# Queue of the two maximum transfers in four attention layers: from SyncE to GpSimd

## The reference

```
logits = einsum('bqhd,bkhd->bhqk', q, k) * scale + bias or mask
w      = softmax(logits)                 # exp(l - max(l)) / sum
out    = einsum('bhqk,bkhd->bqhd', w, v)
```

## Time and profile before

| | |
|---|---|
| median of 3 runs | 2353.46 us (2351.25 to 2359.56) |
| the profiled execution | 2350.0 us, its span 2348.3 us |
| TensorE busy | 2052.1 us, 87% of the span |
| VectorE busy | 1544.7 us, 66% |
| ScalarE busy | 1199.0 us, 51% |
| GpSimd busy | 825.0 us, 35% |
| DMA issues | all by SP; shift_dram<-rows x64 (24 KB), st<-shift_dram x128 (12 KB) |

### The profile page before, as it was taken

The page is one execution under the profiler, slowest core; times in us unless marked ns, Lnnn a source line. Parts: engine busy times, 40 slices in busy tenths (PEclk is TensorE's granted clock), DMA queues, the critical chain, the costliest instruction groups (busy, mean ns, idle before and its releaser), DMA issues. The chain is left out here.

```text
span 2348.3 us, 52692 instructions
## 1 busy us (share of the span) xinstructions
PE 2052.1 (87%) x20735; PEld 1381.5 (59%) x20735; DVE 1544.7 (66%) x2742; ACT 1199.0 (51%) x2044; POOL 825.0 (35%) x1272
## 2 busy tenths in 40 slices
PE   6999999999959997998689989997599985479996
PEld 3666666666648995555578966664345543335553
DVE  5777777777743435666354447774688875768884
ACT  3444444444343324665623326655477776447774
POOL 4444444444423432332144414441233322433330
PEclk9999999999969998999789989998699997769998
DMA  5000000000000022444000214441244420134441
GB/s 167 1 1 1 1 1 1 1 1 1 1 6 2 14 46 70 113 113 99 2 4 1 55 29 113 113 112 32 70 100 115 113 61 1 42 80 107 113 109 46
DMA packets 142787, 120.97 MB, mean 52 GB/s; under 512 B 11808, under 2 KB 127408, under 8 KB 142548
## 3 DMA queue, kind: packets, MB, share of 16 engines
q1 hardware_dynamic: 142548, 117.64, 21.1%
HBM read 63.48 MB, written 54.12 MB: 50 GB/s over the span
## 5 line engine op out<-in xcount | busy, mean ns | idle before, releaser
L906 DVE TENSOR_REDUCE l_group_mx<-maxima 128x4 f32<-128x1024 f32 x248 | 304.0, 1226 | 69.0 <-PE maxima L699 67.5
L834 ACT ACTIVATE l_group_pr<-scores 128x1024 f32<-128x1024 f32 x256 | 261.5, 1021 | 71.7 <-PE scores L720 69.1
L2171 POOL TENSOR_TENSOR l_wide_tiles_sum<-l_wide_pr 128x256 f32<-128x256 f32 x256 | 180.7, 727 | 212.4 <-ACT l_wide_pr L2114 212.4
L2142 DVE RECIPROCAL l_wide_rc<-bank 128x256 f32<-128x256 f32 x128 | 223.8, 1749 | 8.4 <-PE bank L2075 7.9
L2114 ACT ACTIVATE l_wide_pr<-scores 128x512 f32<-128x512 f32 x256 | 139.1, 595 | 163.1 <-PE scores L2058 163.1
L2126 DVE TENSOR_REDUCE l_wide_mx<-maxima 128x2 f32<-128x512 f32 x248 | 159.4, 685 | 52.6 <-PE maxima L2038 52.0
L906 DVE TENSOR_REDUCE l_slope_mx<-maxima 128x6 f32<-128x768 f32 x124 | 118.9, 959 | 74.2 <-PE maxima L706 72.7
L2104 ACT ACTIVATE l_wide_qk<-bank 128x512 f32<-128x512 f32 x128 | 76.4, 597 | 175.2 <-PE bank L2025 175.2
L906 DVE TENSOR_REDUCE l_rope_mx<-maxima 128x6 f32<-128x768 f32 x124 | 118.8, 958 | 56.3 <-PE maxima L706 55.4
L834 ACT ACTIVATE l_slope_pr<-scores 128x768 f32<-128x768 f32 x128 | 103.5, 809 | 87.0 <-PE scores L727 86.8
L834 ACT ACTIVATE l_rope_pr<-scores 128x768 f32<-128x768 f32 x128 | 103.7, 811 | 77.0 <-PE scores L727 76.8
(11 more groups left out here) (468 smaller groups left out, 4853.5 us busy)
## 6 DMA issues: line engine op xcount, KB each, us to landing
l_group_st<-stack_dram SPq DMA_DIRECT2D x64, 384.0 KB, 5.5
l_slope_st<-stack_dram SPq DMA_DIRECT2D x32, 384.0 KB, 5.6
l_rope_st<-stack_dram SPq DMA_DIRECT2D x32, 384.0 KB, 5.5
stack_dram<-l_group_parts SPq DMA_DIRECT2D x64, 192.0 KB, 2.3
stack_dram<-l_group_parts SPq DMA_DIRECT2D x64, 128.0 KB, 1.9
stack_dram<-l_slope_parts SPq DMA_DIRECT2D x32, 192.0 KB, 2.4
stack_dram<-l_rope_parts SPq DMA_DIRECT2D x32, 192.0 KB, 2.3
stack_dram<-l_slope_parts SPq DMA_DIRECT2D x32, 128.0 KB, 2.3
```

The costliest lines, as they stand in the source:

```text
L834: act.activation(pr[:, i % AHEAD, :, 0:keys], Tp[:, :, 0:keys], ACT.Exp).then_inc(s["exps"], 1)
L906: dve.tensor_reduce(mx[:, b % 2, :, :, i], max_bank(i, b)[:, :, 0:BLOCKS * keys].rearrange("p z (a k) -> p z a k", k=keys), AX.X, ALU.max, ...
L2142: own.done(dve.reciprocal(rc[:], Ob[i % 2][:, S:2 * S]))
L2171: pool.tensor_tensor(tiles_sum[:, i % 2, z, :], pr[:, i % 2, z, 0:S], pr[:, i % 2, z, S:2 * S], ALU.add).then_inc(s["added"], 1)
```

## The change

The steps "shift" and "spread" leave SP's lists and are issued by GpSimd, through the same function, with the same waits and semaphores. In slope and rope they follow "parts" of the same period; in group "shift" comes ahead of "reg_q" and "parts", and "spread" after them. High, mid, low and stack stay with SP in their order.

```diff
@@ slope
-            [("parts", 0, 3)],
-            [],
-            [],
+            [("parts", 0, 3), ("shift", 0, 1)],
+            [],
+            [("spread", 0, 1)],
             [],
         ],
         "sp": [
...
-            [("shift", 0, 1), ("high", 0, 3)],
+            [("high", 0, 3)],
             [("mid", 0, 3)],
-            [("spread", 0, 1), ("low", 0, 3)],
+            [("low", 0, 3)],
@@ rope
             [("parts", 0, 3)],
-            [],
-            [],
+            [("shift", 0, 1)],
+            [("spread", 0, 1)],
             [("bias", 0, 1)],
...
-            [("shift", 0, 1), ("high", 0, 3)],
-            [("spread", 0, 1)],
+            [("high", 0, 3)],
+            [],
             [("mid", 0, 3), ("low", 0, 3)],
@@ group
             [("split", 0, 1), ("bias", 0, 1)],
-            [("reg_q", 0, 2), ("parts", 0, 3)],
-            [],
+            [("shift", 0, 1), ("reg_q", 0, 2), ("parts", 0, 3)],
+            [("spread", 0, 1)],
             [("reg_v", 0, 2)],
...
-            [("shift", 0, 1), ("high", 0, 3)],
-            [("spread", 0, 1)],
+            [("high", 0, 3)],
+            [],
             [("mid", 0, 3), ("low", 0, 3)],
@@ pool_piece
-            if what == "split":
+            if what in ("shift", "spread"):
+                sp_piece(pool, what, i, b)
+            elif what == "split":
```

## The result

The changed kernel takes 2619.03 us (median of 4 runs, 2614.16 to 2623.87) against 2352.36 us before: ratio 1.1121, 95% interval 1.11 to 1.1143. That is 267 us slower, in the direction that was forecast, twice the forecast size and outside the range. Its profiled execution has a span of 2616.3 us with a mean granted clock of 0.892, against 2348.3 us and 0.932 before.

A forecast was written before the change was run, and what follows sets the result against it. TensorE's in-order stream sets the time, with a late score 0 paid once a period. Slope 24, rope 33, group 70 make 127 us, plus 8 for layers' last periods: +135, so 2488 us; range 2395 to 2560.

The forecast's parts named there:

- the chain: From GpSimd free for the shift to score 0: shift landing, semaphore, two spreads; 5.70 us in slope and rope.
- The cost d of an issue: Time one transfer issue holds GpSimd, three a period; taken as 1.04 us, the sum moving 168 us per us of d.
- The small power on 128x4: GpSimd instruction on 128x4 elements, nearly all its own software; its 1.04 us was taken as the cost of an issue.
- The landing of the spread: Second spread's start to score 0's weight load: 1.79 us from SP in slope, 2.49 with GpSimd's issue cost.
- rival 4: Gaps of 2 to 3 us a period might lower TensorE's clock: +64, 2552; chance 0.14, shared with a dearer issue.
- Rival 3: SP's queue is the brake; freed, stack lands earlier and TensorE's 27.1 us of waits go: 2327; chance 0.06.
- Rivals 1 and 2: Issues cheap as SP's; 1: landings 0.4 us longer, 2405, chance 0.12; 2: landings as early, 2360, chance 0.08.

## Why the prediction was wrong

**What held.** The direction and its reason: score 0 waits for the spread in nearly every period (57 waits), the stack's waits go, the shift stands where I placed it. Without the collision the chain is the one I drew: in group the shift starts 9.54 us behind score 0 (2453.27 to 2462.81; forecast 9.26), and from the shift to score 0 it is 2470.23 - 2462.81 = 7.42 us (forecast 8.65). The periods of group are 16.9 us in the quiet ones and 17.3 in the mean, against 17.91 forecast and 15.41 before.

**The cost d of an issue.** Taken as 1.04 us, measured 0.51 to 0.57. The small power on 128x4 was the wrong neighbour. This alone would have made the forecast too high, by 168 x 0.5 = 84 us. Group came out 10 us a layer below the forecast; by d alone it would have been 14 x 3 x 0.5 = 21, so other terms took half of that back. The error in d and the one that follows pull in opposite directions, and the total hides a part of the larger one.

**The landing of the spread: the step that failed.** I took 1.79 us from one pair in slope and added 0.70. That row is a landing with the stack not yet issued. I moved the shift, and the spread with it, 2.1 us later and did not ask what SP would be sending by then, though the stack's place stands in my own text and its size, twice 384 KB, on the page. The slope period by its terms:

| term | forecast | measured |
|---|---|---|
| score 0 to the end of parts | 10.57 | 11.7 |
| shift start to spread start | 2.17 | 2.4 |
| first spread's issue | 1.04 | 0.5 |
| second spread to score 0 | 2.49 | 6.5 |
| period | 16.3 | 21.1 |

(measured: score 0 at 1087.47, the shift at 1099.09, score 0 at 1108.53.) The landing is 4.0 of the 4.8 us. Over all periods of slope the medians of the four terms are 11.6, 2.4, 0.5 and 6.3 us. In rope they are 13.3, 2.4, 0.5 and 6.6, against 11.46, 2.17, 1.04 and 2.49: the landing is 4.1 us too long there, and the stretch up to the parts 1.9. Holding the stack back took 123 us from the time, out of the 214 of slope and rope; the later chain and the lower clock go with the rest, and were not parted.

**The clock, rival 4.** I gave it a small chance because a gap of about 2 us in group had kept it at 1.00. In group that held for most periods: between the first and the last shift of a layer the mean is 0.94 and 0.95, against 0.97 before. In slope and rope it is 0.80, down from 0.97 and 0.98:

```profile
906.00:1218.00 312.00, 208.54 (x3064) 134.71 (x3068) 140.09 (x236) 130.10 (x207) 85.27 (x159) 0.80 0.32 73
1495.00:1827.00 332.00, 230.14 (x3182) 153.70 (x3182) 156.18 (x267) 129.33 (x210) 110.23 (x186) 0.80 0.30 69
```

TensorE's extra 59 us of busy time for the same products are what a row shows of its size. So rival 4 was not instead of my forecast but on top of it, in slope and rope. In three of the experiments gaps of 1.8 to 2.1 us in slope were followed by the lower clock too (0.57 in a window behind the gap at 1060.86 in the one with the shift ahead of the parts), where one of 1.9 us in group was not, as these windows around the group's score 0 at 2470.23 show; what else decides it is open.

```profile
2466.00:2470.00 4.00, 2.32 (x30) 1.23 (x26) 3.71 (x8) 1.35 (x3) 2.77 (x5) 1.00 0.54 150
2470.00:2474.00 4.00, 3.72 (x46) 2.15 (x46) 1.91 (x5) 2.75 (x5) 0.00 (x0) 1.00 0.63 119
```

**Rival 3, SP as the brake,** is refuted by the sign. What SP gained in room was worth at most the 27 us of stack waits, which went and were paid for many times over. **Rivals 1 and 2** named issues as cheap as SP's (0.32); it was 0.2 us dearer, so by the cost of the issue alone the truth lay between them and my forecast.

**The rules of the Trainium skill that I weighed.** The Trainium skill, "DMA: Bandwidth & Descriptors", section "Latency and other measured facts", has the first byte of GpSimd's transfers 0.4 us later than SP's. The shifts in group agree: 1.76 us to landing in the median against 1.43. What the Trainium skill, "SBUF — State Buffer", section "SBUF: two separate sides", says of GpSimd's descriptors and VectorE shows in no row here; group's spreads, the ones near that VectorE instruction, landed in 2.1 us in the median. The Trainium skill, "DMA: Bandwidth & Descriptors", has the rule that I should have weighed, in its section "Issuing engines are not separate DMA queues": all transfers run on the same 16 DMA engines and interleave, whoever starts them. The runs agree, and add the price: the second spread of a pair beside the 768 KB takes 6.3 us in slope and 6.5 in rope in the median from GpSimd's queue, and 5.9 and 5.8 right behind the stack in SP's.

**What the packets show, and what stays open.** Why does the small transfer, issued 0.1 us ahead of the stack in a queue of its own, not get through earlier? It could be that its data are moved late, or that they are moved early and only its completion is held until the other writes are done. The trace lists the packets by queue (packets, MB, share of the engines' time; q0 is GpSimd's queue, q1 SP's). In the slope period above, from 1101.5 to 1103.5 us, only SP's packets start, although the first spread was issued at 1101.51:

```profile
q1 hardware_dynamic: 40, 0.16, 39.8%
```

From 1107 to 1108 us the last of the spreads' data are still being moved:

```profile
q0 software_dynamic: 6, 0.01, 4.0%
q1 hardware_dynamic: 4, 0.00, 2.9%
```

The pair consists of six packets of 4 KB. They start at 1104.07, 1104.93, 1104.98, 1105.95, 1107.26 and 1107.54, among the stack's 192 packets of 4 KB (1102.57 to 1107.12) and behind them. In the group period above all six start between 2469.00 and 2469.51. So the data themselves go late: in the 24 periods with the stack at the same moment the last packet starts 5.0 to 6.0 us behind the second spread's issue, in group 1.2 to 2.0 us. A held completion can be only a small part: the landing at 1108.49 is 0.6 us behind the end of the last packet (0.5 to 1.3 in the 24 periods), where the group period has 0.4. Why the DMA engines move these few packets so late stays open; the trace doesn't say which of the 16 moved a packet.

## What to carry to other kernels

When a small transfer on the critical chain is moved, ask first which large ones will be in flight at its new time, and take its landing from a row with that company; moving it to another engine's queue does not part it from them. Sending it first can: 0.37 us ahead in the same queue was enough here, and from GpSimd's queue 1.6 us was, 0.8 us not quite. An engine that is mostly idle is still a bad place for a wait-and-send step if what is queued ahead of it (here 3.8 us of parts) ends later than the data are ready. A gap of 2 us in TensorE's stream can cost more than itself, since the products behind it may run at the lower clock.

## What was not expected of the hardware

- An issue of a plain transfer held GpSimd for 0.50 to 0.57 us in nearly all cases, against 0.23 to 0.40 on SP for the same transfers, and a shift landed 0.3 us later (1.76 us against 1.43 in group).
- 12 KB needed about 6 us beside 768 KB on SP's queue or on GpSimd's, and its 4 KB packets were moved late, not only reported late. 24 KB right behind 384 KB needed 1.9 us in the median and 3.8 at worst.
- Halving the large transfer took the second spread only from 6.3 to 4.3 us in slope and from 6.5 to 4.5 in rope (medians).
- Behind gaps of about 2 us in slope the granted clock was 0.57 to 0.74 in a window of 4 or 5 us, while in the group period shown, with a gap as long, it stayed at 1.00.
